# Second attention of a gated cross-attention block: six PSUM banks for scores, and one bank shared by the query chain and the output chain

## The reference, cut to what matters

```python
def _L1_xattn_ref(x, cond, Wq, bq, Wkv, bkv, Wp, bp):     # x: layer norm of the rows; cond: 512 context rows
    q = (x @ Wq + bq).reshape(1, B * N, H, hd)             # 16 heads of 16 channels
    kv = (cond @ Wkv + bkv).reshape(1, -1, 2, H, hd)
    ...
    q = _fq_sym(q * scale, axis=-1)      # rounded to integers -127..127 times a scale per row and head
    k = _fq_sym(k, axis=-1)
    v = _fq_sym(v, axis=2)
    attn = softmax(q @ k^T)              # every token against all 512 context rows
    attn = _fq_unsigned(attn, axis=-1)   # rounded to 0..255 of its largest
    out = attn @ v
    return out @ Wp + bp                 # added to x with tanh(g_xattn[1]) in front
```

## Time and profile before

| what | value |
|---|---|
| time, 3 runs | median 893.65 us (889.62 to 894.23) |
| the profiled execution | 896.02 us, span 894.3 us |
| second attention, first largest to last exponential | 369.2 to 594.6 us of the span |
| busy over the span | TensorE 81%, VectorE 77%, ScalarE 51%, GpSimd 55% |
| TensorE's granted clock over the span | 0.87 of full speed |

### The profile page before, as it was taken

One profiled execution on the slowest core, in us unless ns is written; L12 is line 12 of the kernel. 1 busy time (PEld: TensorE's weight loads), 2 busy tenths in 40 slices (PEclk: granted clock), 3 DMA queues, 4 the chain that ended last, 5 costly groups with the idle time before them and its releaser, 6 DMA issues. The chain is left out here.

```text
span 894.3 us, 18300 instructions
## 1 busy us (share of the span) xinstructions
PE 724.3 (81%) x5700; PEld 492.9 (55%) x5701; DVE 684.2 (77%) x1804; ACT 453.5 (51%) x1049; POOL 492.4 (55%) x610
## 2 busy tenths in 40 slices
PE   3468856778898999577778777868869999999995
PEld 1257744446676555244444444344548888885663
DVE  4968956766676567799998989977858888886776
ACT  3355424413342454498888889965314444442331
POOL 5285797356662787954445644600047544477770
PEclk8678975869999999689786978678969999999999
DMA  8024444733443331399999999971025544455332
GB/s 307 1 70 138 149 160 160 219 101 113 139 149 126 95 88 29 84 197 176 176 181 168 182 179 198 164 174 45 7 58 164 155 141 144 145 173 175 98 100 94
DMA packets 203263, 121.24 MB, mean 136 GB/s; under 512 B 146476, under 2 KB 194480, under 8 KB 203184
## 3 DMA queue, kind: packets, MB, share of 16 engines
q1 hardware_dynamic: 192816, 91.10, 42.5%
q0 software_dynamic: 10368, 29.14, 11.8%
HBM read 64.16 MB, written 32.98 MB: 109 GB/s over the span
## 5 line engine op out<-in xcount | busy, mean ns | idle before, releaser
L1481 DVE TENSOR_SCALAR_CACHE_REDUCE sb_wk<-PS 128x512 f16<-128x512 f32 x256 | 161.7, 683 | 11.4 <-PE PS L1343 11.3
L710 POOL DMA_INDIRECT sb_xnf<-token_table,sb_ids x110 | 106.4, 967 | 110.6 <-DVE sb_ids L624 52.6
L271 PE MATMUL PS<-sb_xnT,sb_sgu 128*128 128x512 f16 x528 | 127.1, 394 | 1.1 <-DVE sb_lg L481 0.6
L271 PE MATMUL PS<-sb_region,sb_wkh 128*128 x720 | 121.9, 321 | 2.4 <-issue 2.0
L1432 ACT ACTIVATE sb_wkh<-PS,sb_slotv 128x512 int16<-128x512 f32 x128 | 87.3, 702 | 13.4 <-DVE sb_wk L1481 10.5
L271 PEld LDWEIGHTS PS<-sb_region,sb_wkh 128*128 128x128 f16 x720 | 71.2, 100 | 39.0 <-issue 5.4
L1432 ACT ACTIVATE sb_xnf<-PS,sb_slotv 128x512 int16<-128x512 f32 x128 | 87.0, 707 | 9.6 <-DVE sb_wk L1481 6.6
L879 ACT ACTIVATE sb_wk<-PS 128x512 f32<-128x512 f32 (+1 forms) x48 | 28.6, 596 | 119.4 <-PE PS L271 107.0
L271 PEld LDWEIGHTS PS<-sb_xnT,sb_sgu 128*128 128x128 f16 x528 | 52.4, 100 | 59.0 <-issue 8.1
L795 PE MATMUL PS<-sb_sdn,sb_wkh 128*128 128x256 f16 x544 | 71.5, 284 | 13.4 <-DVE sb_wkh L981 12.2
L1010 DVE SCALAR_TENSOR_TENSOR sb_wk<-PS,sb_sm,sb_wk 128x176 f32<-128x176 f32 x120 | 42.6, 396 | 46.2 <-ACT sb_wk L907 46.0
(11 more groups left out here) (299 smaller groups left out, 1664.9 us busy)
## 6 DMA issues: line engine op xcount, KB each, us to landing
slot_table<-sb_wa SPq DMA_DIRECT2D x60, 256.0 KB
slot_table<-token_table SPq DMA_DIRECT2D x16, 640.0 KB
sb_stg<-gu SPq DMA_DIRECT2D x24, 352.0 KB, 4.7
sb_stg<-dn SPq DMA_DIRECT2D x24, 256.0 KB, 3.2
token_table<-sb_xnf SPq DMA_DIRECT2D x16, 256.0 KB, 4.8
sb_stg<-sgu SPq DMA_DIRECT2D x8, 352.0 KB, 5.3
sb_x_sb<-x SPq DMA_DIRECT2D x1, 2048.0 KB, 12.1
out<-sb_x_sb SPq DMA_DIRECT2D x16, 128.0 KB, 1.8
```

The source lines that it names most:

```text
L271: last = nc.tensor.matmul(out_, lhs(i, c), rhs(j, c), start=(c == 0 and n == 0 and not begun), stop=(c == C - 1 and n == 2 and not more))
L710: nc.gpsimd.indirect_dma_start(xg[l][g % XR[l]][:, n, :], None, xw[l][:, :], bass.IndirectOffsetOnAxis(ap=ids[:, 2 * g + n:2 * g + n + 1], ...
L1481: nc.vector.tensor_scalar(h_any[(2 * s + h) % 6], PS[:, (2 * s + h) % LB, :], LEVELS, None, ALU.add, ALU.min, accum_out=h_nb[s % 3][:, h:h ...
```

## The change

- The ring of scores has six banks (0 to 5).
- `o_bank` and `q_bank` are both bank 7, and the averages of even and odd tiles share bank 6. So the two chains must alternate in bank 7, and the averages of a tile must wait until the tile before is divided. New waits: `query_transposes` for the update of the output before (`o_x`), `output_transposes` for the quotients of the group two ahead (`q_frac`), `weighted` at a tile's first pair for all tiles before (`o_norm`, t in place of t-1).
- `weighted_at`: the averages of a tile's first pair are done one step later, together with those of its second.
- Offsets: from the fourth group on the query chain starts at place 14, with its products still at places 1 and 2, the largest at 4, scales 4 (from 5), quotients 5 (from 6), parts on GpSimd 7 to 10 (from 8 to 11), turns of the integers 11 and 12 (from 9 and 11), copies 12 and 13 (from 10 and 12). For the first group the copies move from steps 13 and 15 to 14 and 15. The output chain moves by one place: turn 6, high half 7, low half 9, products 9 and 10, update 12.

```diff
-        AHEAD, BEHIND, LB = 2, 4, 5
+        AHEAD, BEHIND, LB = 2, 4, 6
...
-        o_bank, q_bank = PS[:, 5, :], PS[:, 7, :]
-        w_bank = PS[:, 6, 0:D], PS[:, 5, 0:D]
+        o_bank = q_bank = PS[:, 7, :]
+        w_bank = PS[:, 6, 0:D], PS[:, 6, D:2 * D]
...
         def query_transposes(pe, t):
             at_least(pe, q_int, 0, t + 1)
+
+            at_least(pe, o_x, 0, t // 2 - 1)
             if t % 2:
                 at_least(pe, q_ready, 0, t)
...
-        ROWS, TO_PE, HIGH_Q, LOW_Q, PRODUCTS, LARGEST, SCALES, FRACTIONS, PARTS, BACK, COPIES = 0, 0, 2, 4, 4, 7, 8, 9, 11, 12, 13
+        ROWS, TO_PE, HIGH_Q, LOW_Q, PRODUCTS, LARGEST, SCALES, FRACTIONS, PARTS, BACK, COPIES = 0, 0, 1, 3, 3, 6, 6, 7, 9, 13, 14
 
         def chain_start(G):
 
-            return max((GSTEPS - 1) * (G - 1), GSTEPS * (G - 1) - 3)
+            return max((GSTEPS - 1) * (G - 1), GSTEPS * (G - 1) - 2)
...
+        def weighted_at(w):
+
+            if w > 0 and w % PAIRS == 0:
+                return ()
+            return (w - 1, w) if w > 1 and w % PAIRS == 1 else (w,) if w >= 0 else ()
...
                 if pair == 0:
-                    at_least(pe, o_norm, 0, t - 1)
-                    if t % 2:
-                        at_least(pe, o_x, 0, t // 2)
+                    at_least(pe, o_norm, 0, t)
...
             def output_transposes(o):
                 at_least(pe, o_norm, 0, 2 * o + 2)
-                at_least(pe, o_x, 0, o)
+
+                at_least(pe, q_frac, 0, min(o + 3, GROUPS))
...
-                if s >= BEHIND:
-                    weighted(s - BEHIND)
+
+                for w in weighted_at(s - BEHIND):
+                    weighted(w)
...
-                    G = query_step(s, BACK + 2 * j)
+                    G = query_step(s, BACK + j)
...
-                o = output_step(s, 5)
+                o = output_step(s, 6)
...
-                    o = output_step(s, 8 + j)
+                    o = output_step(s, 9 + j)
...
-                    G = query_step(s, COPIES + 2 * j)
+                    G = query_step(s, COPIES + j)
...
-                o = output_step(s, 6)
+                o = output_step(s, 7)
...
-                o = output_step(s, 8)
+                o = output_step(s, 9)
...
-                o = output_step(s, 11)
+                o = output_step(s, 12)
```

## The result

| | before | after |
|---|---|---|
| time, 5 runs each | median 893.65 us (889.62 to 895.47) | median 898.99 us (896.67 to 902.17) |
| ratio to before, 95% interval | | 1.0067 [1.0038, 1.0095] |
| the profiled execution | 896.02 us, span 894.3 | 897.82 us, span 896.1 |
| start of the first largest to start of the last exponential | 224.7 us | 225.7 us |
| VectorE idle in that stretch | 18.3 us | 18.9 us |

The change makes the kernel 0.7% slower, 5.3 us on the medians. The forecast was 893.2, no change. In a second set of runs, six of the kernel after and eleven of the kernel before, the ratio was 1.0087 [1.0061, 1.0114]; its profiled execution had a span of 901.9 us, 229.1 of them in that stretch with VectorE idle for 22.6. A single profile differs from the next by more than the change is worth; so I use the profiles for where waits sit, and the medians for what they cost.

The account below looks back on a forecast made before the run. The second attention was taken to run at VectorE's pace, ScalarE close behind, with 11.0 us of waits reachable. Terms -3.3 - 2.2 + 0.8 + 1.6 + 2.0 + 0.7 = -0.4 us gave 893.2 us, range 886.5 to 900.

Parts of the forecast that it names:

- Averages of a tile's first pair: Place 12: DMA turns wait for the later averages, 0.4 times 1 us in five groups, +2.0 us (0 to 10); place 5 free.
- rival B: Late DMA turn of place 12 delays ScalarE; queries' largest waits 1.7 us more in six groups; 899.7 us, chance 0.20.
- Update: VectorE's update of five outputs: sixth bank frees scores 0.66 us earlier, leaving waits of 0.1 to 0.6; -3.3 us (0 to -5.2).
- Scores at place 4: VectorE's waits for scores and queries' largest at place 4 shrink by 0.66 us each; -2.2 us (0 to -4.5).
- First group: Step 18's wait of 1.28 us goes, but the copy moved to ScalarE's step 14 costs about 1.25; these cancel, 0.
- Turns of the integers: Direct sequence behind the update delays the scores of place 15 by 0.15 us in each of five groups; +0.8 us.
- ScalarE's lag: ScalarE 1.85 us behind at the next place 0, delaying the queries' largest, 0.8 us each at steps 80 and 96; +1.6 us.
- idle over 1 us before the first copy of a group: Sign of the forecast: ScalarE idle over 1 us before a group's first copy (L1264) in most groups.
- End of the stage: Turn of step 124 waits for the division and averages, delaying the next branch's routing; +0.7 us (0 to 1).
- Outside 366 to 600 us: Nothing is edited outside this stretch, so it should not change; if it does, the forecast is wrong throughout.
- A: Sixth bank wins: ScalarE's lag stays covered, turns land in time, some 8.5 of 11.0 us go; 886.6 us, chance 0.28.
- C: VectorE waits for TensorE's products, not the ring; at most 3.2 us gained, costs of 5.1 stay; 895.6 us, chance 0.10.

Follow-up runs that it names:

- the late averages: Kernel before with both tiles' averages in bank 6, those of a tile's first pair one step later and behind the division: 902.93 us, ratio 1.0140.
- the moved step alone: Kernel before with the averages of a tile's first pair one step later, in their old banks, without the new wait for the division: 902.77 us, ratio 1.0104.
- the change with six turned buffers: Changed kernel with six buffers of turned weights in place of four: 891.08 us, ratio 0.9978.
- the shared chains with six: Kernel before with both chains in bank 7 at their new places, five banks of scores, plus six buffers of turned weights: 892.84 us, ratio 0.9992.

## Why the prediction was wrong

The step that failed is "**Averages of a tile's first pair** ... I put it at 0.4 times 1 us in each of five groups, +2.0 us", with its last sentence "At place 5 the same wait costs nothing". Measured on the kernel before the same edit costs 11.6 us (902.93 against 891.35), which is over the term's own upper bound of 10 even without the 0.7 for the end of the stage that it holds too, and the later step alone 9.7 (902.77 against 893.09). The mechanism was named rightly, down to its place: a later issue, and slow landings that lose their cover. The size was off by a factor of about five. The parts add up to the whole within the noise: 11.6 less 5.5 for the sixth bank, and 0 for the chains, is 6.1, between the 5.3 and the 8.4 us that the two sets measured for the whole change. The traces show two reasons for the size, and suggest a third.

- *The turns are later than I worked out.* From VectorE's start of a step to the issue of its turn, the mean at place 12 went from 3.0 us to 6.2 (steps 28 to 108); I had about 5. At place 4 it went from 3.9 to 5.6 (steps 20 to 116), where I had counted 0.9 of delay and a cost of nothing. The late averages come twice in 16 steps, and I charged them once.
- *The queue catches up slowly.* A turn takes 1.3 us of the queue and a step of ScalarE at full pace 1.33, so the turns behind a late one are late too; only because VectorE's mean step is 1.8 us does the delay fade. In the changed kernel the mean issue after the second exponential is 3.3, 2.7, 2.0 and 2.2 us at places 12 to 15 (steps 20 to 120), and 2.5, 2.3, 1.8, 1.6 and 1.4 at places 4 to 8. I wrote this down under rival B and did not carry it into the sum, which has one turn per group and not four. The turns of places 5 and 13, issued a mean 1.6 and 1.0 us after their second exponential before, came 2.3 and 2.7 us after it. The exponentials that start right at the landing of the turn they wait for rose from 13 to 27 of 124.
- *It may feed itself.* The circle of steps 88 to 96 above: late landing, late exponential, late copy, late turn of integers, late averages, late DMA turn. I followed each link once, and not round. For it: the turns of place 12 are issued 6.2 and 6.0 us after VectorE's start in the two profiles of the change, and 4.7 and 5.0 with the late averages or the moved step alone, where the integers' turns stand earlier. No run takes this link away by itself, so its share is not shown.

The other terms:

- *Update, -3.3 us*: its wait fell by 4.0 us in one profile and by 3.7 in the other, but not by the bank. It falls as far with five banks and the chains at their new places (1.2, 0.8 and 1.0 us in three kernels). Of this term the moved chains are shown, the 0.66 us of the sixth bank is not. The idle time of the whole place fell by 3.5 us in one profile and by 1.3 in the other, so other waits came in its stead. On the five outputs that the term counted (5.2 us before) 2.2 and 2.7 are left, but the output of step 28, which had no wait before, has 1.0 and 1.4.
- *Scores at place 4, -2.2*: 3.4 fell away at the place in one profile and 0.8 came to it in the other; with the chains alone, on five banks, all 4.5 fell away. The profiles don't price the bank here. By the medians it is worth 5.5 us on the kernel with late turns, as much as both terms together, but that agreement is luck: the terms were worked out for a kernel whose turns are in time. There its worth wasn't run alone: the change with six turned buffers and the shared chains with six, which has five banks, have ratios of 0.9978 and 0.9992, and their intervals overlap.
- *First group, 0*: wrong by a microsecond. The copies at steps 14 and 15 hold back the scores of steps 16 and 17, and VectorE waits there 2.3 us in place of the 1.28 at step 18:

```profile
398.55 0.69 DVE L1489 TENSOR_SCALAR_CACHE_REDUCE sb_wk<-PS 128x512 f16<-128x512 f32 x1 [1.65 <-ACT sb_xnf L1440]
...
400.47 0.69 DVE L1489 TENSOR_SCALAR_CACHE_REDUCE sb_wk<-PS 128x512 f16<-128x512 f32 x1 [0.61 <-PE PS L1351]
```

- *Turns of the integers, +0.8, and ScalarE's lag, +1.6*: the medians show nothing for the chains alone, though place 15 costs 2.0 us there and not 0.8, paid for by the gains above. In the whole change place 15 costs 4.2 us (3.0 in the second profile), and 0.8 once the turns have spare buffers. ScalarE was to be idle over 1 us before the first copy of a group; it was idle 1.8 us before all of them together, since it came to them late.
- *End of the stage, +0.7*: from the start of the last exponential to the last landing 6.3 us against 5.7, as said; the last turn is issued 2.9 us after VectorE's last largest began, against 1.9.
- *Outside 366 to 600 us*: unchanged. The stage begins 0.8 us later and what follows the last landing is 0.5 shorter, on an unedited program.

Of the rivals, B had the right price (899.7) and the right place of origin, and the wrong victim: the queries' largest, at which it would show by over 8 us, waits 0.1 us in one profile and 2.6 in the other. The lateness came out as waits for scores, at places 9, 12 and 15 in the first profile and at 4, 12 and 15 in the second. So the agreement of its price is in part luck. A is refuted by ScalarE's waits for turns, which were to stay near 5 us; its gains (8.5 us) show in one profile at 6.9 and in the other at 0.5. C, by which the products and not the ring are what VectorE waits for, was right in that the ring wasn't what held the update; it is wrong for the whole kernel, where the ring's sixth bank is worth 5.5 us and the costs came to more than its 5.1.

The rule of the Trainium skill that the forecast weighed (Perfetto Trace Analysis, Matmuls: independent matmul groups should rotate through different PSUM banks) agrees with the 5.5 us that the sixth bank is worth on the kernel with late turns. Its reverse, two groups in one bank, doesn't carry the loss: with six turned buffers the averages share a bank at no cost that can be measured (0.9987 against 0.9986). What the change gave up was not a bank but a step of a buffer's life.

## What to carry to other kernels

When a consumer moves later, find every producer that waits for it before it may overwrite its input, and compare the delay with the slack of that queue. Here a turn takes 1.3 us of the queue and comes every 1.33 us at the producer's full pace, 1.8 on average, so one delay was passed on to three or four turns before it faded. Take the slow landings into the count and not the median alone. Count each such delay in all places where the moved work occurs, and follow it round the ring until it comes back to where it began. Where a rearrangement costs more than its parts explain, one spare buffer in the loop is a cheap test: if the loss goes with it, it was the buffer. And profile a changed kernel twice before the waits of single places are read as its gains: here one profile showed 6.9 us and the next 0.5.

## What the runs showed of the hardware

In every version 23 to 34 of the 128 turns take over 4 us to land (median 3.3 to 3.4). In the trace of the kernel before three stretches around such landings show the same hole. The DMA view of 546 to 548 us, in 40 slices of 0.05 us (busy share in tenths, then GB/s):

```profile
DMA  9999999999900000000000101010000000000099
GB/s 640 241 302 241 297 256 266 227 256 251 10 0 0 0 0 0 0 0 0 0 0 0 10 5 10 5 10 10 10 10 10 5 10 10 10 10 5 20 246 282
...
q8 instruction: 1, 0.02, 3.4%
```

For 1.3 us the engines move next to nothing, with a turn in flight, and the one packet of another queue in this window is a fetch of instructions of 16 KB. The windows that begin at 496.5 and 512 us look alike, the second with a further fetch, of 8 KB. The turns in flight at the start of the three holes took 4.5 to 5.2 us to land. Counted over all 13 traces: of the 379 turns that took over 4 us, 344 had such a packet of instructions, of 8 or 16 KB, in flight within 3 us of their issue, and of the 1285 others 269. The loads of weights don't sort them so: in the trace before 18 of the 32 slow turns had one in flight, and 59 of the 96 others. That the fetch is the cause is not tested; no run changed the fetches. Such landings were covered before by the slack ahead of the turns of place 12 (issued 3.0 us after VectorE's start, where it is 6.2 after).
